# Self-attention contexts gathered four heads to a bank: one reciprocal per four heads instead of per two, and a different pairing of the value and row-sum products

## The reference

```python
probs = jax.nn.softmax(scores, axis=-1)             # 16 heads, 256 x 256
ctx = jnp.einsum('bhqk,bhkd->bhqd', probs, V)       # 32 channels per head
ctx = ctx.transpose(0, 2, 1, 3).reshape(B, S, D)
out = jnp.einsum('bsd,df->bsf', ctx, W_out)
return out + X

def weight_quant(w):                                # w1, w3, w2 of the feed-forward layer
    scale = 1.0 / jnp.clip(jnp.mean(jnp.abs(w)), EPS)
    return jnp.clip(jnp.round(w * scale), -1.0, 1.0) / scale
```

## Time and profile before

| | |
|---|---|
| device time, median of 3 runs | 576.0 us (575.85 to 577.02) |
| the profiled execution | 576.91 us, its span 575.0 us |
| mean granted TensorE clock in it | 0.979 of full speed |
| PE matmul busy over the span | 530.1 us (92%) |
| DVE busy over the span | 482.6 us (84%) |
| ACT, POOL busy | 363.4 us (63%), 153.4 us (27%) |

### The profile page before, as it was taken

How to read it: one execution, slowest core, us unless ns; L and a number is a source line. 1 busy time by engine, 2 the same in 40 slices (tenths; PEclk the granted TensorE clock), 3 DMA queues, 4 the chain that set the end, 5 groups by cost and what they waited for, 6 DMA issues and landing times.

```text
span 575.0 us, 9999 instructions
## 1 busy us (share of the span) xinstructions
PE 530.1 (92%) x3799; PEld 352.6 (61%) x3803; DVE 482.6 (84%) x716; ACT 363.4 (63%) x442; POOL 153.4 (27%) x186
## 2 busy tenths in 40 slices
PE   7999955789999999999999999999989998996896
PEld 3876722356666666666666666666667773454442
DVE  3588796899989999999999999999977366489986
ACT  1133460978788688687786886887885334896142
POOL 2359943101112202202102102201000001598401
PEclk9999996999999999999999999999998998999799
DMA  8998127599999999999999999999999989100001
GB/s 315 338 364 255 63 49 174 159 203 196 201 193 204 200 190 204 210 212 210 206 199 205 203 196 203 197 201 205 196 194 181 273 358 395 82 0 1 1 0 38
DMA packets 287806, 107.41 MB, mean 187 GB/s; under 512 B 276896, under 2 KB 277920, under 8 KB 286368
## 3 DMA queue, kind: packets, MB, share of 16 engines
q1 hardware_dynamic: 287776, 107.01, 85.6%
HBM read 37.26 MB, written 0.52 MB: 66 GB/s over the span
## 4 chain that ended last, share of the span: by engine, by line
PE 63%; DVE 18%; DMA 5%; issue 5%; ACT 4%; POOL 4%; SPq 0%; DVEq 0%; ACTq 0%
PE ps L646 16%; PE ps L648 8%; PE ps L628 8%; PE ps L630 8%; PE ps L629 8%; DMA pT<-split 4%; PE ps L748 4%; DVE rows L1233 3%; POOL qrope L480 2%; DVE split L1215 2%; DVE qrope L1265 2%; DVE qrot L1271 1%; DVE KL L1253 1%; PE ps L677 1%; PE ps L850 1%
## 5 line engine op out<-in xcount | busy, mean ns | idle before, releaser
L646 PE MATMUL ps<-pT,VH 128*128 128x256 f16 x1024 | 196.8, 274 | 1.9 <-DMA pT<-split 1.9
L648 PE MATMUL ps<-pT,VL 128*128 128x128 f16 x1024 | 183.4, 220 | 0.0
L1233 DVE TENSOR_SCALAR_CACHE_REDUCE rows<-ps,qback 128x1024 f32<-128x1024 f32 x128 | 163.6, 1280 | 17.5 <-PE ps L630 16.8
L1003 ACT ACTIVATE split<-rows,rz 128x2048 f16<-128x2048 f32 x64 | 124.8, 1995 | 67.5 <-DVE rz L1184 67.4
L1215 DVE SCALAR_TENSOR_TENSOR split<-rows,rz,split 128x2048 f16<-128x2048 f32 x64 | 150.3, 2350 | 1.3 <-issue 1.2
L989 ACT ACTIVATE rows<-rows,negm 128x2048 f32<-128x2048 f32 x64 | 127.2, 1988 | 0.2 <-DVE negm L1238 0.2
L646 PEld LDWEIGHTS ps<-pT,VH 128*128 128x128 f16 x1024 | 100.5, 98 | 42.8 <-DMA pT<-split 4.9
L648 PEld LDWEIGHTS ps<-pT,VL 128*128 128x128 f16 x1024 | 100.6, 98 | 27.3
L628 PE MATMUL ps<-KH,qcur 128*128 128x512 f16 x256 | 97.8, 382 | 14.0 <-DVE qcur L1290 10.7
L509 POOL TENSOR_TENSOR ctx_c<-acc 128x128 f32<-128x128 f32 x32 | 24.4, 762 | 296.8 <-ACT acc L978 296.8
L629 PE MATMUL ps<-KL,qcur 128*128 128x512 f16 x256 | 97.5, 381 | 0.0
(11 more groups left out here) (172 smaller groups left out, 656.1 us busy)
## 6 DMA issues: line engine op xcount, KB each, us to landing
w_sb<-w SPq DMA_DIRECT2D x3, 2816.0 KB, 15.8
wq_sb<-wq SPq DMA_DIRECT2D x4, 1024.0 KB, 8.6
wo_sb<-wo SPq DMA_DIRECT2D x16, 256.0 KB, 4.5
wkcq_sb<-wkcq SPq DMA_DIRECT2D x4, 768.0 KB, 9.3
keys<-ctxT SPq DMA_DIRECT2D x8, 256.0 KB, 7.7
stage<-ctxT SPq DMA_DIRECT2D x16, 128.0 KB, 8.0
stage<-kcos SPq DMA_DIRECT2D x8, 256.0 KB, 7.8
stage<-ksin SPq DMA_DIRECT2D x8, 256.0 KB, 9.3
```

Of the source, the lines that this page charges most:

```text
L646: nc.tensor.matmul(bank(6 + r % 2, 0, 256), VH[:, 4 * b + k, :], p.rearrange("p x q -> p (x q)"), start=(b == 0 and k == 0), stop=False)
L648: last = nc.tensor.matmul(bank(6 + r % 2, 0, 128), VL[:, 4 * b + k, :], p[:, 0, :], start=False, stop=(b == 7 and k == 3))
L1003: nc.scalar.activation(split[:, split_slot(r, half), :, 0, :], rows[:, k, half * 2048:(half + 1) * 2048].rearrange("p (b k) -> p b k", k=1 ...
L1233: nc.vector.tensor_scalar(rows[:, k, c * 1024:(c + 1) * 1024], ps[:, score_bank(s) * 512:(score_bank(s) + 2) * 512], qback[:, r // 2:r // ...
```

## The change

- The two units of a group now share one bank: V products in columns 0 to 255 of bank 2 + g % 2, the sums in columns 256 to 511, each head's sum in its own 32 partitions. context_out(g) makes one reciprocal and one multiplication on 128 partitions for four heads. For the last group both are split in two halves of 128 tokens, and the output projection of tile 0 waits only for the first of them.
- head_products(v) now makes the V products of unit v and the ones products of unit v - 1; there are nine calls instead of eight. The first has only V products, the last only ones products.
- pT holds three units instead of two, at another address.
- context_out(0), (1), (2) stand in DVE's rounds v = 3, 5, 7, and context_out(3) after the loop.
- ACT makes the first two pieces of the sum over w2 in round 0, and one each in rounds 1 and 2. weight_total(2) moves from round 3 to round 2 on DVE, weight_sum(2) and weight_scale(2) from round 4 to round 3 and to bank 3.
- On DVE the clip of w1b moves from round 5 to round 4, and that of w3b from behind the loop into round 6. That of w2b stays last.

```diff
-        pT = at("pT", B + 23 * KB, [128, 4, TT, TOK])
+        pT = at("pT", C + 20 * KB, [128, 6, TT, TOK])
+        PT_UNITS = 3
...
             def head_products(v):
                 g, first = v // 2, v % 2 * 2
-                wait(pe, cT_done, v - 1)
-                if v == 0:
-                    pe.wait_ge(v_copied, 2)
-                if v in (0, 4):
-                    pe.wait_ge(wmean_done, v // 4 + 2)
-                for x in range(2):
-                    pe.wait_ge(pT_done[x], v + 1)
-                o = (2 + v % 2) * 512 + g % 2 * TOK
+                if v < UNITS:
+                    if first == 0:
+                        wait(pe, cT_done, g - 1)
+                    if v == 0:
+                        pe.wait_ge(v_copied, 2)
+                    if v in (0, 2):
+                        pe.wait_ge(wmean_done, v // 2 + 2)
+                    for x in range(2):
+                        pe.wait_ge(pT_done[x], v + 1)
                 for k in range(TT):
-                    for x in range(2):
-                        a = first + x
-                        nc.tensor.matmul(ps[a * DH:(a + 1) * DH, o:o + TOK],
-                                         v_sb[:, k, (4 * g + a) * DH:(4 * g + a + 1) * DH], pT[:, a, k, :],
-                                         start=(k == 0), stop=(k == TT - 1), tile_position=(0, a * DH))
-                    for x in range(2):
-                        a = 2 - first + x
-                        last = nc.tensor.matmul(ps[a * DH:(a + 1) * DH, o:o + TOK], ones[:, 0:DH], pT[:, first + x, k, :],
-                                                start=(k == 0), stop=(k == TT - 1), tile_position=(0, a * DH))
+                    if v < UNITS:
+                        for x in range(2):
+                            a = first + x
+                            last = nc.tensor.matmul(ps[a * DH:(a + 1) * DH, (2 + g % 2) * 512:(2 + g % 2) * 512 + TOK],
+                                                    v_sb[:, k, (4 * g + a) * DH:(4 * g + a + 1) * DH],
+                                                    pT[:, v % PT_UNITS * 2 + x, k, :],
+                                                    start=(k == 0), stop=(k == TT - 1), tile_position=(0, a * DH))
+                    if v >= 1:
+                        u = v - 1
+                        o = (2 + u // 2 % 2) * 512 + TOK
+                        for x in range(2):
+                            a = u % 2 * 2 + x
+                            last = nc.tensor.matmul(ps[a * DH:(a + 1) * DH, o:o + TOK], ones[:, 0:DH],
+                                                    pT[:, u % PT_UNITS * 2 + x, k, :],
+                                                    start=(k == 0), stop=(k == TT - 1), tile_position=(0, a * DH))
...
-                if v == 4:
-                    pe.wait_ge(cT_done, 3)
-                    weight_sum(2, bank(2, 0, 1))
+                if v == 3:
+                    weight_sum(2, bank(3, 0, 1))
...
             head_products(UNITS - 1)
+            head_products(UNITS)
...
-                    if t == 0:
-                        pe.wait_ge(cT_done, 2 * g + 2)
+                    if t == 0 or g == FG - 1:
+                        pe.wait_ge(cT_done, g + t + 1)
...
-                if v < 4:
-                    abs_sum(2, v)
+                if v == 0:
+                    abs_sum(2, 0)
+                if v < 3:
+                    abs_sum(2, v + 1)
...
-            def context_out(v):
-
-                g, own, other = v // 2, v % 2 * 64, 64 - v % 2 * 64
-                o = (2 + v % 2) * 512 + g % 2 * TOK
-                dve.wait_ge(aav_done, v + 1)
-                link(nc.vector.reciprocal(arz[own:own + 64, v % 2, :], ps[other:other + 64, o:o + TOK]))
-                nc.vector.tensor_tensor(cT[own:own + 64, g, :], ps[own:own + 64, o:o + TOK], arz[own:own + 64, v % 2, :],
-                                        ALU.mult).then_inc(cT_done, 1)
+            def context_out(g):
+
+                o = (2 + g % 2) * 512
+                dve.wait_ge(aav_done, 2 * g + 3)
+                for part in ([slice(0, TOK)] if g < FG - 1 else [slice(t * 128, (t + 1) * 128) for t in range(TT)]):
+                    n = part.stop - part.start
+                    link(nc.vector.reciprocal(arz[:, g % 2, part], ps[:, o + TOK + part.start:o + TOK + part.start + n]))
+                    nc.vector.tensor_tensor(cT[:, g, part], ps[:, o + part.start:o + part.start + n], arz[:, g % 2, part],
+                                            ALU.mult).then_inc(cT_done, 1)
...
-                if v in (0, 4):
-                    weight_scale(v // 4 + 1, bank(2, 0, 1))
+                if v in (0, 3):
+                    weight_scale(v // 3 + 1, bank(2 + v // 3, 0, 1))
                 if v + 2 < UNITS:
                     maxima(v + 2)
-                if v == 3:
+                if v == 2:
                     weight_total(2)
-                if v == 5:
-                    clip(0, w1b)
-                if v >= 1:
-                    context_out(v - 1)
-            context_out(UNITS - 1)
-            clip(1, w3b)
+                if v in (4, 6):
+                    clip(v // 2 - 2, (w1b, w3b)[v // 2 - 2])
+                if v in (3, 5, 7):
+                    context_out(v // 2 - 1)
+            context_out(FG - 1)
             clip(2, w2b)
```

More of the change, by code:

```diff
@@ L1081, in probabilities_out @@
                 wait(act, aav_done, v - 1)
-                nc.scalar.activation(pT[:, v % 2 * 2 + 1].rearrange("p k t -> p (k t)"), bank(1), ACT.Copy)\
+                nc.scalar.activation(pT[:, v % PT_UNITS * 2 + 1].rearrange("p k t -> p (k t)"), bank(1), ACT.Copy)\
                     .then_inc(pT_done[1], 1)
@@ L1370, in probabilities_out @@
                 wait(dve, aav_done, v - 1)
-                nc.vector.tensor_copy(pT[:, v % 2 * 2].rearrange("p k t -> p (k t)"), bank(0)).then_inc(pT_done[0], 1)
-            def context_out(v):
-                g, own, other = v // 2, v % 2 * 64, 64 - v % 2 * 64
-                o = (2 + v % 2) * 512 + g % 2 * TOK
-                dve.wait_ge(aav_done, v + 1)
-                link(nc.vector.reciprocal(arz[own:own + 64, v % 2, :], ps[other:other + 64, o:o + TOK]))
-                nc.vector.tensor_tensor(cT[own:own + 64, g, :], ps[own:own + 64, o:o + TOK], arz[own:own + 64, v % 2, :],
-                                        ALU.mult).then_inc(cT_done, 1)
+                nc.vector.tensor_copy(pT[:, v % PT_UNITS * 2].rearrange("p k t -> p (k t)"), bank(0)).then_inc(pT_done[0], 1)
+            def context_out(g):
[6 more added lines that the diff above has]
+                                            ALU.mult).then_inc(cT_done, 1)
             def clip(j, wb):
```

## The result

Before 576.0 us, after 581.22 us (medians of five runs each, 575.84 to 577.76 and 579.37 to 581.74); ratio 1.0072, 95% interval 1.005 to 1.0094. The change costs some 4 us by the ratio, 5 by the medians, where I forecast 3.4 us saved. The profiled execution took 581.17 us, its span is 579.3, the mean granted clock 0.976.

A forecast was written before the change was run, and what follows sets the result against it. DVE, gapless from the w2 total to the last unit's copy, was taken as the bound; that copy 2.6 us earlier and the projection 3.4 earlier gave 576.0 - 3.4 = 572.6 us, range 571.0 to 575.3.

The forecast's parts named there:

- the price of the clips under POOL's cover: DVE's w1b and w3b clips beside POOL's w2 pieces: 2.15 us each, bounds 1.63 and 1.63 + 0.85.
- Other edits: pT's new address with three units, and weight scale 2 at about 519.3, giving POOL 2 us: worth nothing each.
- Total to copy of unit 7: DVE from the w2 total at 518.1 to that copy: 15.47 us, copy at 533.6 against 536.17.
- The projection: Output projection on PE, after the copy of unit 7 and products(7) and (8): starts about 536.05 against 539.48.
- the time of a reciprocal follows columns: DVE contexts on 128 partitions: reciprocal 1.755 and multiplication 0.422, so 2.18 us for four heads.
- f: Rival: reciprocals cost by elements, two contexts on the path 2.18 dearer each; 578.1 us, chance 0.02.
- ACT's two pieces in a row: ACT in round 0: two w2-sum pieces take 1.5 each, exponentials of unit 2 at 511.34, 1.0 late.
- the wait of 1.6: DVE's w2 total waits for ACT's last piece, from 516.5 to 518.1: 1.6 us.
- (d): Rival: V and ones products in two banks do not run side by side; 2.5 us more, 575.1, chance 0.06.
- PE stays later than DVE's layer norm: Before the feed-forward transposes: layer norm path ready at 545.6, PE's filling matmuls end at 547.0.
- (c): Rival: clock falls from 529.5 to 534.3, last two product steps at 1.2 GHz; 1.72 more, 574.3, chance 0.14.
- (e): Rival: low clock reaches the projection's tile 0, 4.3 us on top of (c); 578.6, slower, chance 0.06.

The follow-up runs named there:

- e4: Kernel after with the clips where the kernel before has them (w1b in round 5, w3b behind the last context): 582.55 us, 1.0101 of the kernel before.
- e5: Kernel after with a small unused reduction on DVE ahead of the w1b clip: 583.43 us, 1.0116 of the kernel before.
- e10: Kernel after with POOL waiting for the first context before w2, w1b clip between contexts 2 and 3, w3b and w2b last: 574.4 us, 0.995 of before.
- e14: Kernel after with POOL waiting for the first context before w2, w1b clip in round 7, w3b clip last: 575.7 us, one run.
- e15: Kernel after with POOL waiting for the first context before w2, two unused reductions and the w1b clip in round 7, w3b last: 574.46 us, one run.
- e7: Kernel after with POOL waiting for the first context before it starts on w2: 572.62 us, 0.9926 of the kernel before.
- e9: Kernel after with POOL waiting for the maxima of unit 4 before rounding w3, no gap ahead of w2: 572.44 us, 0.9916 of the kernel before.
- e13: Kernel after with each POOL w2 piece waiting on a semaphore for the end of the one before: 571.59 us, 0.9914 of the kernel before.
- e1: Kernel after with the w1b and w3b clips behind the last context, ahead of the w2b clip: 572.99 us, 0.9936 of the kernel before.
- e3: Kernel after with POOL waiting for the w1b clip before it scales w2: 572.7 us, 0.9937 of the kernel before.
- e8: Kernel after with the w1b and w3b clips behind the last context, w2b behind the first tile's quantising: 571.67 us, 0.9899 of the kernel before.

## Why the prediction was wrong

**The step that failed** is the price of the clips under POOL's cover: "so I take 2.15 twice, with 1.63 as the lower bound and, if a clip has to wait out a whole piece of POOL, 1.63 + 0.85 above". Measured were 11.75 and 1.62. The upper bound took for granted that DVE gets in at the next end of a piece. That is what the clip at 528.90 had shown, and what the rule of the Trainium skill that I weighed says (SBUF — State Buffer, Who interferes with whom: whoever comes first has the pair for the whole instruction). It held for every clip that came within 7.5 us of a gap (1.62 to 2.23 us). In six kernels where POOL had been gapless for 8.2 us or more (after, e4, e5, e10, e14, e15) every end of a piece passed without the clip getting in, and it ended 1.47 to 1.49 us behind POOL's last one; the rule has no word on this, and the measurement decides.

**The step that let it in** is under "Other edits": the weight scale of w2 at 519.3 instead of after POOL's end, "Nothing each". I costed what POOL gains and did not ask what its idle time had been good for. It was the gap of 1.88 us through which the w1b clip got in, 5.2 us later. e4 (no gap, old place of the clips: 9.39) and e7 (gap of 0.74, new places: 1.62 and 1.97) show this from both sides.

**The sum with the right price.** Total to copy of unit 7: forecast 15.47, measured 23.68 (540.69 - 517.01). The clips account for 9.07 more (11.75 + 1.62 against 4.30). The rest is 0.86 less: the sixteen rows of this stretch add up to 24.55, 0.87 more than the stretch, since neighbouring rows overlap, and my sum took them as they stand. e7 shows the same error without the shut-out clip: the stretch takes 13.92 (532.77 - 518.85), 0.71 less by its clips and 0.84 less by the rest. The projection then follows 3.2 after that copy instead of 2.45; the last transposes run at 1.2 GHz (1.86 instead of 1.06), and the products of unit 6 come behind them. Together 9.0 late, as L854 shows, and 8.6 in the medians (581.22 against 572.6).

**Right, by the rows of the kernel after:** the time of a reciprocal follows columns, as the rotation's does (f out); ACT's two pieces in a row, and the wait of 1.6; pairs of products in two banks start 0.02 apart (514.08, 514.10), so (d) is out; PE stays later than DVE's layer norm (in the kernel after the transposes at 554.77 wait for nothing). With the clips in the forecast's places and let through, that stays so (e7, e9, e13: no wait). Where all three clips stand ahead of the layer norm, DVE is the later one (a wait of 1.36 in e1). Rivals (c) and (e) have the right sign, the wrong cause: the clock fell while PE stood for 10.26 us behind the clip, and it was back by 541.18, before the projection. No rival has a clip that is shut out.

**Open.** That POOL's queue runs further ahead of its engine while nothing holds it, and so keeps DVE out from some point on, fits e9, e14 and e13, but no trace shows it directly. Where the border lies, and whether it goes by time, by the number of pieces or by their kind, is open too. What is shown is that the clip's wait costs the time (e1, e3), and that idle time or a semaphore wait in POOL's stream removes it (e7, e9, e13).

## What to carry to other kernels

Before an idle gap of an engine is closed, look at what another engine does just behind it: here one instruction got in only there. A duration read once under contention is a sample and no bound; ask what releases it in the worst case, here the end of the other engine's whole queue. Where POOL streams long beside DVE's bf16 tensor_scalar, break its stream (here a wait of 0.7 us within 7.5 us ahead, or a semaphore between pieces, did it), or keep such instructions out of it: e13 and e8 stand at 0.9914 and 0.9899 of the kernel before, and so (over 1.0072) some 1.6 and 1.7% below the kernel after.

## What the runs showed of the hardware that I had not expected

- A DVE clip (tensor_scalar, 128x5632 bf16, SBUF to SBUF) of 1.62 us took 4.69 to 11.75 us in five kernels, and 2.93 in one where POOL's end was near, each time until 1.47 to 1.49 us after the end of POOL's gapless stream; POOL's pieces were not stretched (6.65 and 5.98 with or without it).
- With an idle gap of POOL (0.74 to 4.02 us) 7.5 us ahead or less, the same clip took 1.62 to 2.23 us, and POOL paid some 1.4 us for it.
- A tensor_reduce of 3.08 us on the same tile, in the same place, was not held up.
- When PE resumed at 535.53 after 10.26 us without work, the granted clock was 0.50 (1.2 GHz), and it was back at 0.99 in 541 to 543: transposes took 1.94 us instead of 1.06.
